# A third pair of split buffers in the factor stream of a conditional residual and recurrence kernel

## The reference, cut to what matters

```python
h = gelu(c @ W1 + bias1, approximate=False)          # c: layer norm of cond, 16 x 512
w = h @ W2 + bias2                                   # 16 x 16384
a1, b1, a2, b2 = [t.reshape(B, D, R) for t in jnp.split(w, 4, axis=-1)]
u = jnp.einsum('btd,bdr->btr', x, a2)
mid = gelu(jnp.einsum('btd,dl->btl', x, base_down) + jnp.einsum('btr,blr->btl', u, b2), approximate=False)
v = jnp.einsum('blr,btl->btr', b1, mid)
out = jnp.einsum('btl,kl->btk', mid, base_up) + jnp.einsum('bkr,btr->btk', a1, v)
x = x + (x + out)
...
next_h = jnp.tanh(xw_t + prev_h @ Wh)                # 512 steps, xW = x @ Wx + b
```

## Time and profile before

| | |
|---|---|
| median of 3 executions | 1379.74 us (1379.56 to 1380.09) |
| the profiled execution | 1381.67 us, its span 1380.0 us |
| PE, DVE, ACT busy over the span | 95%, 70%, 49% |
| mean granted TensorE clock | 0.966 of full speed |
| W2 stream | first cast at 17.17 us, last low ends at 160.59 us |

### The profile page before, as it was taken

The page is one execution under the profiler, slowest core; times in us unless marked ns, Lnnn a source line. Parts: engine busy times, 40 slices in busy tenths (PEclk is TensorE's granted clock), DMA queues, the critical chain, the costliest instruction groups (busy, mean ns, idle before and its releaser), DMA issues.

```text
span 1380.0 us, 49753 instructions
## 1 busy us (share of the span) xinstructions
PE 1309.1 (95%) x20524; PEld 1056.3 (77%) x20524; DVE 970.9 (70%) x3757; ACT 683.0 (49%) x2467; POOL 254.6 (18%) x525
## 2 busy tenths in 40 slices
PE   6786789999999999999999999999999999999996
PEld 4332478888888888888888888888888888888764
DVE  5665755777777777777777777777777777767564
ACT  5654424555554555555455554545455555544442
POOL 1000011221222222222222221212121222222111
PEclk9777789999999999999999999999999999999998
DMA  8878510112120212121212121111112121101011
GB/s 283 264 246 231 164 27 9 25 25 41 20 40 16 48 18 48 18 42 24 40 25 41 25 38 29 33 29 31 31 25 41 26 41 19 24 3 33 3 33 32
DMA packets 292273, 75.66 MB, mean 55 GB/s; under 512 B 273072, under 2 KB 273088, under 8 KB 292048
## 3 DMA queue, kind: packets, MB, share of 16 engines
q1 hardware_dynamic: 292048, 72.49, 23.9%
HBM read 55.68 MB, written 16.78 MB: 53 GB/s over the span
## 4 chain that ended last, share of the span: by engine, by line
PE 81%; DVE 7%; ACT 5%; issue 3%; DMA 3%; SPq 0%; POOL 0%; DVEq 0%; ACTq 0%; POOLq 0%
PE bulk L857 38%; PE rec L878 28%; PE bulk L846 7%; PE bulk L860 4%; PE bulk L831 2%; ACT hf L522 2%; DVE act_s L603 2%; DMA work<-in_L_cond_W_dram 2%; DVE act_s L695 2%; ACT rec L479 1%; DVE z L720 1%; DVE work L690 1%; ACT act_s L501 1%; DMA work<-in_L_cond_base_down_dram 1%; DVE mid_s L603 0%
## 5 line engine op out<-in xcount | busy, mean ns | idle before, releaser
L878 PEld LDWEIGHTS rec<-hs,wh_s 128*128 128x128 f16 x16352 | 442.5, 96 | 129.8 <-DVE hs L728 124.6
L522 ACT ACTIVATE hf<-z,scl 128x32 f32<-128x32 f32 x1024 | 273.5, 314 | 536.9 <-DVE z L720 531.5
L878 PE MATMUL rec<-hs,wh_s 128*128 128x32 f16 x16352 | 493.8, 177 | 7.8 <-ACT rec L479 4.3
L415 POOL TENSOR_TENSOR work<-work,hf 128x64 f32<-128x64 f32 x512 | 244.1, 477 | 947.4 <-DVE hs L728 947.4
L720 DVE TENSOR_REDUCE z<-rec 128x32 f32<-128x96 f32 x1024 | 230.7, 256 | 148.6 <-PE rec L878 140.4
L725 DVE TENSOR_SCALAR hs<-hf 128x32 f16<-128x32 f32 x1024 | 182.4, 178 | 101.1 <-ACT hf L522 101.0
L857 PE MATMUL bulk<-mid_s,up_s 128*128 128x512 f32 x768 | 222.8, 413 | 0.0
L728 DVE SCALAR_TENSOR_TENSOR hs<-hf,hs 128x32 f16<-128x32 f32 x1024 | 196.8, 192 | 35.3
L857 PE MATMUL bulk<-act_x,down_s 128*128 128x512 f32 x768 | 220.4, 410 | 0.0
L857 PE MATMUL bulk<-act_s,wx_s 128*128 128x512 f32 x768 | 208.9, 409 | 0.0
L479 ACT ACTIVATE rec<-work 128x32 f32<-128x32 f32 x1024 | 184.3, 210 | 0.0
(11 more groups left out here) (115 smaller groups left out, 1035.5 us busy)
## 6 DMA issues: line engine op xcount, KB each, us to landing
work<-in_L_cond_W_dram SPq DMA_DIRECT2D x33, 1024.0 KB, 5.8
work<-in_x_dram SPq DMA_DIRECT2D x256, 64.0 KB, 3.4
out_dram<-work SPq DMA_DIRECT2D x256, 64.0 KB, 2.3
work<-in_L_cond_base_up_dram SPq DMA_DIRECT2D x1, 1024.0 KB, 6.1
work<-in_L_cond_base_down_dram SPq DMA_DIRECT2D x1, 1024.0 KB, 8.1
work<-in_L_cond_Wx_dram SPq DMA_DIRECT2D x1, 1024.0 KB, 5.1
work<-in_L_cond_Wh_dram SPq DMA_DIRECT2D x1, 1024.0 KB, 5.3
bias2T<-in_L_cond_bias_dram SPq DMA_DIRECT2D x4, 16.0 KB, 3.7
```

The lines of the kernel that those rows point to most:

```text
L415: nc.gpsimd.tensor_tensor(xs, xs, hf[:, t % 4], ALU.add).then_inc(sum_done, 1)
L522: nc.scalar.activation(hf[:, t % 4, half], z[:, half], ACT.Tanh, scale=inv).then_inc(tanh_done, 1)
L878: last = nc.tensor.matmul(R[fo][:, m, 0:PARTS, :], wh_s[:, q, k, n * P:(n + 1) * P], hs[:, k, :, :], start=(m == k == q == 0), stop=(k == ...
```

## The change

The split buffers become three (`act_s`, `mid_s`, `wx_s`), and the waits for a buffer reach back three halves instead of two. The number of halves by which the casts run ahead in ScalarE's program stays two. VectorE takes the remainder of a factor one half later, after the low of the next even half and ahead of the next factor's sum. The bias is added to `fac` in two operations of 128 elements for each partition, where there were four of 64.

```diff
-        w2_s = (act_s, mid_s)
+        w2_s = (act_s, mid_s, wx_s)
...
             def w2_high(n):
 
                 arrived(act, W2_ENTRY + n)
-                if n >= 2:
-                    act.wait_ge(row_hi, n - 1)
-                    act.wait_ge(w2_lo, n - 1)
-                nc.scalar.copy(w2_s[n % 2][:, HI].rearrange("p k n -> p (k n)"), w2_raw(n)).then_inc(w2_hi, 1)
+                if n >= 3:
+                    act.wait_ge(row_hi, n - 2)
+                    act.wait_ge(w2_lo, n - 2)
+                nc.scalar.copy(w2_s[n % 3][:, HI].rearrange("p k n -> p (k n)"), w2_raw(n)).then_inc(w2_hi, 1)
...
                 dve.wait_ge(w2_hi, n + 1)
-                if n >= 2:
-                    dve.wait_ge(row_mm, n - 1)
-                dst = w2_s[n % 2].rearrange("p s k n -> p s (k n)")
+                if n >= 3:
+                    dve.wait_ge(row_mm, n - 2)
+                dst = w2_s[n % 3].rearrange("p s k n -> p s (k n)")
...
                 pw = fsum[:].rearrange("p r (g b) -> p g b r", g=GROUPS)
-                bias = bias2T[:, q, dt:dt + 1, :].broadcast_to([P, GB, RANK])
+                bias = bias2T[:, q, dt:dt + 1, :].rearrange("p (o a) r -> p o a r", o=1).broadcast_to([P, GROUPS, GB, RANK])
                 for rep in range(REPS):
-                    for g in range(GROUPS):
-                        last = nc.vector.tensor_tensor(f[:, g, rep], pw[:, g], bias, ALU.add)
+                    last = nc.vector.tensor_tensor(f[:, :, rep], pw, bias, ALU.add)
                 last.then_inc(fac_done, 1)
...
             for n in range(2, HALVES):
                 w2_low(n)
+                if n >= 6 and n % 2 == 0:
+                    split_factor(n // 2 - 3)
                 if n >= 4 and n % 2 == 0:
                     factor(n // 2 - 2)
-                if n >= 5 and n % 2:
-                    split_factor(n // 2 - 2)
+            split_factor(LAST - 2)
```

More of the change, by code:

```diff
@@ L831, in _ @@
                         last = nc.tensor.matmul(bulk[0:2 * B, BANK_ROW + n % 2, :], h_s[:, k].rearrange("p s b -> p (s b)"),
-                                                w2_s[n % 2][:, part, k, :], start=(part == HI and k == 0),
+                                                w2_s[n % 3][:, part, k, :], start=(part == HI and k == 0),
                                                 stop=(part == LO and k == KT - 1))
```

## The result

The changed kernel takes 1357.89 us in the median of 4 executions (1356.65 to 1358.43), the kernel before 1379.91 in 4. The ratio is 0.9836, with a 95% interval of 0.9819 to 0.9853: 22.0 us or 1.6% faster. The profiled execution has a span of 1356.7 us, where the one before had 1380.0, so the two traces differ by 23.3. Two executions behind these pages were slow, one of the kernel before (2175.82 us) and one of the version with x spread over the stream (1597.87 us, without which the median of that version is 1350.95 us and not 1351.64), and the ratios leave both out.

The account below looks back on a forecast made before the run. It took a latency ring of low, cast, rounding and remainder to pace the W2 stream; 19.2 us before the x transfers plus 7.8 in the tail make 27.0 us off 1379.74, forecast 1353 us, range 1348.5 to 1361.

Parts of the forecast that it names:

- the ring of waits: W2 stream before the change: low, cast into the same buffer, rounding, remainder, low; paces each pair of halves at 8.49 us.
- three signs of being wrong: Casts wait for landings mid-stream; granted clock stays at 0.50 to 0.75; low(26) does not follow x by 21.7 us.
- rival 1: W2 stream: four raw slots replace the split buffers as bound, 6.7 us per pair, 1357.7 us in all; chance 0.22.
- What bounds the kernel now: W2 stream: latency of a closed chain between VectorE and ScalarE, no engine full, 8.49 us per pair.
- The third buffer and the later remainder: Steady W2 stream: both waits covered by lows, leaving VectorE's own work as a floor of 5.66 us per pair.
- The bias: VectorE, per factor: two operations of 128 elements cost 0.46 us, ends 0.35 and 0.68, saving 0.24 us.
- What is late next: Middle of W2 stream: 6.1 us per pair, between VectorE's 5.66 and the 6.4 of casts 2 to 7.
- the loop over four slots: Raw W2 slots: landing, cast and low before reuse; 4.9 us per pair at 5.5 us landings, 6.7 at 9.0.
- rival 2: TensorE at 1.2 GHz: pairs of 8.7 us give 1376.7 us, half of them 1363.6; chance 0.08 for both.
- The start: First halves of W2: low(7) ends at 48.7 us, 2.4 earlier; low(21) then ends at 91.4, 19.2 us earlier.
- The x transfers keep that gain: SyncE's queue: cast 26 follows the end of low(21) by 21.7 us in either kernel, so the 19.2 us stay.
- The tail: End of W2 stream, from cast 26: last low ends 7.8 us earlier, pairs near the 5.66 us floor.

## Why the prediction was right, and where it was off

The forecast of 1353 was 4.9 us too low, in the range, with the sign right. What it said of the ring of waits, and of opening it, was right. What it said of the bound that comes next was not: of its three signs of being wrong, two came. Casts wait for landings through the middle (11.4 us in 13 waits, rival 1 at 0.22), and cast 26 follows the end of low(21) by 23.7 us, not 21.7. Remainders also still wait for the rounding behind the first one, which it had excluded. By its own steps:

- **What bounds the kernel now.** Right. The ring of low, cast, rounding and remainder paced the pairs: the late remainder or the third buffer alone opens it, half of the bytes or a fifth slot leave it at 8.5 us. One thing I passed over. The granted clock of TensorE was 0.76 over the seven pairs before, and is 1.00 over those after, so a part of the gain could be the clock's. Two rows of the kernel before, in one of its three long pairs (8.75 us): four matmuls, from the chain that ended last, and the cast that comes late behind them:

```profile
73.15 1.91 PE bulk L831 x4
```

```profile
77.00 1.90 ACT L432 CAST mid_s<-work 128x2048 fp32r<-128x2048 f32 x1 [1.33 <-PE bulk L831]
```

In the next pair, a short one (8.33 us), the same four take 1.11 us and the cast at 85.34 waits 1.03, starting 0.15 us after the low ahead of it ends. So matmuls at the lower clock cost some 0.3 to 0.4 us in each of the three long pairs. An estimate from these rows is 1 to 2 us of the 14.8 that the seven pairs gained; no run held the clock at one level.
- **The third buffer and the later remainder.** That the ring's own waits would be covered was right. The 0.6 to 1.4 us before a remainder that are left stem from casts that wait for landings, and with the fifth slot one wait of 0.3 us is left. I costed them together and did not say that one would do. The late remainder alone has all of the gain that can be measured with four slots.
- **The bias.** Taken as 0.46 for two, measured 0.57, inside the ends of 0.35 and 0.68. With four slots the difference does not show in the time.
- **What is late next.** Here the sum is off, and the bound is another. I took a pair of 6.1 us, a value between VectorE's row and the pace of casts 2 to 7 that no mechanism stands behind, and it is 6.38: 7 x 0.28 = 2.0 us. I had the loop over four slots with landings of 5.5 (hidden) and 9.0 (the bound, 6.7), and gave the second 0.22. The landing is 7.5 in the mean, between them, and the loop is the bound, with 1.1 us of waits in it for which I had put 0.1. TensorE's clock, rival 2, is at 1.00 as in the row from 20 to 40 us.
- **The start.** Low(7) ends at 47.69, not 48.7: 1.0 us better, as cast 6 started at 39.09 and not at 40.20. Low(21) ends at 92.36, 18.2 earlier instead of 19.2.
- **The x transfers keep that gain.** They kept it but for 2.0 us. From the end of low(21) to cast 26 it is 116.06 - 92.36 = 23.7 us, not 21.7. I held that stretch to be fixed by the queue's order, but its length is not fixed: the 16 transfers took 15.52 us to issue, 2.5 more than before, and half 26 landed 0.5 us sooner behind its own issue. In the other traces the 16 took 13.02 us with a pair of 6.91, 14.36 with four bias operations, 15.68 with the late remainder alone, and 10.40 and 11.22 with half of the bytes.
- **The tail.** 20.6 us from cast 26 to the end of the last low, where it was 28.3: 7.7 us, predicted 7.8.

Together 18.2 - 2.0 + 7.7 = 23.9 us earlier at the end of the stream (160.59 to 136.62 is 24.0). What follows it is 0.7 longer (1220.1 against 1219.4 us), the cause of which stays open, and the span is 23.3 shorter. The profiled execution before lay 1.8 us over its median and the one after 0.5 over, which leads to the 22.0 of the medians.

The agreement of 1357.9 with the 1357.7 of rival 1 is partly chance: its pair was 6.7, and the x transfers made up for that. Its mechanism is what the fifth slot showed. That 1353 came within 4.9 us is luck in part as well, since 6.1 stood for another bound.

The figure from the Trainium skill ("DMA: Bandwidth & Descriptors", Bandwidth), 341 GB/s for a 1 MB transfer, is an estimate of 6.15 us for a pair. The page has that figure from transfers issued by GpSimd; here SyncE issues them. The stream ran at 325 to 329 GB/s with four slots and at up to 370 with five, so the page's rate is no limit here. That 6.15 lies near 6.38 confirms nothing. Neither the page's figure nor my row of 2.66 us set the pair: the number of slots did.

## What to carry to other kernels

When a stall is between two engines of which neither is full, list what is queued ahead of the releasing instruction, and move the waiting one behind work that is ready anyway: here a few moved lines did it with the two buffers that were there, and on top of it a third was worth something only once the slots were no longer the bound. After opening such a ring work out each other loop over a fixed number of buffers with the landing at the new pace, which lay between the two landings that the trace before had shown, and with the small steps that the loop passes. And treat a burst of small transfers in the middle of a stream as a stall with a length of its own: spreading it gained 6.9 us here with four slots and 3 with five.

## What the runs showed of the hardware that I had not expected

The share for which the transfer engines count as busy hardly tells how much they could still move. At 0.97 with four slots it was 325 to 329 GB/s, at 1.00 to 1.03 with five it was 355 to 370. And the time that SyncE needs to issue the same 16 transfers of 64 KB differs with what else is in flight: 10.40 us in the changed kernel with half of the W2 bytes, 15.52 with all of them, and 13.01 in the kernel before, where the W2 loads come further apart.
